# One sequence of hop groups, hop products head by head, and mix turned inside the base product, in an mLSTM attention and expert FFN kernel

## The chip, the cores and the metric

The kernel runs on one core of a Trainium2 chip. The metric is device time in microseconds, from start to end of one execution; the median of three runs of the kernel before is 4010.18 us.

## What is computed

For 32 batches of 512 queries and contexts of width 512, eight heads of 64: the query tokens are normalized; keys and values come from the context. The part that matters here is the hop term. Every pair (v, m) of positions has its own embedding row, looked up in a table of 2017 rows by an index matrix, and each query is multiplied with the rows of its 512 partners, head by head:

```python
pos_emb = rpe[hops]                                   # 512 x 512 indices, rows of 512
pe = pos_emb.reshape(Sq, Sq, NH, DH)
k_hop = jnp.einsum('bhvc,vmhc->bhvm', qh, pe)
qk = jnp.einsum('bhsd,bhtd->bhst', qh, k_scaled)
C = (qk + k_hop) * D                                  # D: causal decay, zero for m > v
normalizer = jnp.maximum(jnp.abs(jnp.sum(C, axis=-1, keepdims=True)), jnp.exp(-max_log_D))
h = (C / (normalizer + EPS)) @ vh                     # then a layer norm per head
```

Behind it stands a feed-forward part on x plus the attention output: a layer norm, a base product of 512 x 512, and a router that picks two of ten experts from ten scores and weights a low-rank product of rank 16 for each of eight true ones (128 columns in all). These weighted 128 columns are called mix; mix times a 128 x 512 matrix is added to the base product.

## The kernel before

All engines run their own list of instructions, tied together by semaphores. The span has a setup (to about 43 us), the hop stage (43 to about 1600 us) and the batch loop.

**The hop stage** computes k_hop for all batches at once and stores it in DRAM (hop_products). A group is four queries v with all 32 batches, 128 rows. Queries fall into four tiles of 128 (s = 0 to 3), each tile into four quarters of 32 (c) and each quarter into eight groups (k), 128 groups in all. Only partners m up to the query are needed, so a group of tile s has s full tiles of 128 partners for each of its four queries, and on the diagonal c + 1 tiles that hold 32 partners of each of the four queries. Its width is 128 s + 32 (c + 1) columns.

For each such tile GpSimd issues one indirect DMA (L661 for full tiles, L654 for diagonal ones) that gathers 128 table rows of 2 KB. Full tiles of query v go to rows[v], one buffer set of three tiles for each v; diagonal ones to rows_diag, two sets taken by the parity of c. GpSimd waits until PE has turned the former content. PE transposes each gathered tile in four instructions (L1246) into one of three PSUM banks; VectorE and ScalarE copy the tiles in turn (L484 diagonal, L487 full) to rowsT. Then the product of query v (L1261): the weights are the normalized queries of the group, turned by PE (L1215) and copied by ScalarE in two halves (L760) into q_diag, in which each pair of heads stands as a block of 64 columns with zeros in the rows of the other head. Four matmuls of 128 rows and 64 columns (a float32 matmul is two instructions) write two PSUM banks, which VectorE and ScalarE copy to hop_out (L496); SP stores hop_out in two DMAs for each group.

The order of a group is written out in hop_order: its diagonal tiles, the full tiles of queries 0 and 1, then product v followed by the full tiles of query v + 2. The statistics and the norm of the next group's queries (L953 to L960, L733, L735) stand in the same order. x of the group two ahead is loaded by four DMAs on SP (L525), queued behind the stores of the group before. hop_segments runs the four tiles s as four segments one after another, each with stages and semaphores of its own (pe_h, dve_h, act_h, gathered); at a seam GpSimd waits until the last tile of the segment before has been turned, and PE until its last copies are made. Inside a segment the order is k, then c.

**The batch loop** runs 32 batches as overlapping rounds of 12 steps. In a step PE forms scores of a unit (L1332), adds the hop products by transposing them into the same banks (L1340), weighs values with the unit before (L1356), and does the preparation of the next batch and the FFN of the one before between. SP loads the hop products (hop_load) for pairs of heads. DVE's router (L1119 to L1143) ends in mix; PE turns mix (turn_mix, L1373), ScalarE copies it to mixT (L898), and base (L1387, eight instructions, then L1389 with mixT, two) forms the base product. Four of these, t = 0 to 3, fall in each round. In the steps of BASE, turn_mix stands ahead of turn_context(2), turn_queries(0) and base. ScalarE runs in order: behind the copy to mixT stand the exponentials of the next unit (L810), which GpSimd masks (L687, L683) and DVE multiplies with the scores (L1054).

Of the kernel before, what the change touches and what calls it, by code (L numbers as in the profile page):

```python
# [52 lines left out]

class TwoRounds:
# [26 lines left out]
def build(nc, x, ctxt, hops, igate_w, igate_b, fgate_w, fgate_b, rpe, ln_w, ln_b,  # L81
# [14 lines left out]

# [23 lines left out]
    with ExitStack() as ctx:  # L120
# [38 lines left out]
        q_diag = [place(KT * VG * 2 * B) for _ in range(2)]  # L159
# [72 lines left out]
        act_q = Stage(sem("act_q"), ["ln", "rstd", "lo", "hi"])  # L232
        gathered = [[sem(f"gathered{s}_{v}") for v in range(VG)] for s in range(ST)]
        gathered_diag = [[[sem(f"gathered_diag{s}_{i}_{j}") for j in range(3 + i)] for i in range(2)] for s in range(ST)]
# [6 lines left out]
        def turn_steps(s, c, v):  # L241
            return [("turn", c, v, t) for t in range(s)]

        def diag_steps(c):
            return [("diag", c, j) for j in range(c + 1)]

        def hop_order(s, c):

            order = diag_steps(c) + turn_steps(s, c, 0) + turn_steps(s, c, 1)
            for v in range(VG):  # L250
                order.append(("prod", c, v))
                if v + 2 < VG:
                    order += turn_steps(s, c, v + 2)
            return order

        quarters = range(QUARTERS)


        turned_tiles = [[o for c in quarters for o in hop_order(s, c) if o[0] != "prod"] for s in range(ST)]
        turned_number = [{o: n for n, o in enumerate(ts)} for ts in turned_tiles]  # L260

        def evacuated_by(s, step, part):
            return step[0] == "prod" or turned_number[s][step] % 2 == part

        def turn_bank(s, step):
            return bank(TURN_BANKS[turned_number[s][step] % len(TURN_BANKS)])

        def bank_before(s, step):

            n = turned_number[s][step]  # L270
            n_banks = len(TURN_BANKS)
            if n >= n_banks:
                return turned_tiles[s][n - n_banks], 0
            return [o for m, o in enumerate(turned_tiles[s]) if m % n_banks == n][-1], 1

        pe_h, dve_h, act_h = [], [], []
        for s in range(ST):
# [155 lines left out]
        block = ctx.enter_context(nc.Block())  # L433


        def segment_over(engine, s, *stages):

            if s:
                for st in stages:
# [11 lines left out]
        def hop_segments(engine, body, apart=(ST - 1,), begin=None):  # L451

            for s in range(ST):
                if begin:
                    begin(s)
# [1008 lines left out]
```

## Time and profile before

| | |
|---|---|
| median of three runs | 4010.18 us (4005.64 to 4011.32) |
| profiled execution, time | 4004.49 us |
| its span | 4002.8 us |
| mean granted clock of PE | 0.954 of full speed |
| busy over the span | PE 86%, DVE 66%, ACT 46%, POOL 51% |
| moved | 813.64 MB, mean 203 GB/s |

The profiled execution is read for all durations. The span is what the rows below count from 0; the time is 1.7 us more. Matmuls of a line overlap each other, so for PE the busy time of a group divided by its count is the cost of one in the stream, and the mean of one is its latency. Indirect DMAs on POOL are the time in which GpSimd issues them.

### The profile page before, as it was taken

The numbers are of one execution on the slowest core, as the hardware profiler recorded it, in microseconds if no ns is written. First come the engines' busy times: TensorE is split into PE (matmuls) and PEld (weight loads), VectorE is DVE, ScalarE is ACT, GpSimd is POOL, SyncE is SP. The second block draws the span as 40 slices with busy tenths as digits, with TensorE's granted clock in tenths as the row PEclk, the third lists the DMA queues.
The fourth block names the chain that finished last, engine by engine and source line by source line (L and its number), as shares of the span: only waits on it lengthen the run. The fifth ranks groups of instructions, "written<-read, shape, count | busy, mean of one in ns | idle before, by whom it ended". The sixth has DMA issues, their size and how long they took to land.

```text
span 4002.8 us, 62357 instructions
## 1 busy us (share of the span) xinstructions
PE 3430.6 (86%) x20788; PEld 2029.9 (51%) x20788; DVE 2628.1 (66%) x5500; ACT 1838.8 (46%) x4353; POOL 2054.3 (51%) x2247
## 2 busy tenths in 40 slices
PE   4677878888788888589999999999999999999997
PEld 3555555555455454345555555555555555555543
DVE  5444545555444444477877888878888788887874
ACT  2444444444344444344444454545545455454441
POOL 2356667777777776134444444444444444444443
PEclk7789989999999999799999999999999999999998
DMA  5678889999899998455554544555545554555541
GB/s 143 194 225 285 290 268 328 326 339 335 289 335 326 331 329 302 143 160 146 148 151 143 161 138 139 168 152 157 144 140 166 151 159 142 145 164 147 166 120 36
DMA packets 409649, 813.64 MB, mean 203 GB/s; under 512 B 100314, under 2 KB 204762, under 8 KB 407284
## 3 DMA queue, kind: packets, MB, share of 16 engines
q1 hardware_dynamic: 322292, 524.36, 42.7%
q0 software_dynamic: 87040, 285.28, 22.1%
q8 instruction: 171, 2.80, 0.3%
q14 instruction: 146, 1.20, 0.1%
HBM read 632.67 MB, written 176.69 MB: 202 GB/s over the span
## 4 chain that ended last, share of the span: by engine, by line
PE 41%; DVE 21%; DMA 14%; issue 8%; ACT 6%; POOL 5%; SPq 4%; DVEq 0%; ACTq 0%; POOLq 0%
PE psum L1387 11%; PE psum L1261 7%; DMA arena<-in_L_xattn_rpe_dram,arena 6%; PE psum L1246 5%; DMA arena<-in_x_dram 5%; POOL arena L661 4%; DVE arena L1054 4%; PE psum L1340 4%; PE psum L1332 3%; PE psum L1310 3%; DMA arena<-hop_products 3%; PE psum L1389 3%; PE psum L1279 2%; SPq L525 2%; ACT arena L810 2%
## 5 line engine op out<-in xcount | busy, mean ns | idle before, releaser
L661 POOL DMA_INDIRECT arena<-in_L_xattn_rpe_dram,arena x768 | 730.0, 951 | 290.5 <-issue 180.6
L1246 PE MATMUL psum<-arena 128*128 128x128 f32 x4352 | 619.5, 291 | 230.6 <-DMA arena<-in_L_xattn_rpe_dram,arena 126.7
L1246 PEld LDWEIGHTS psum<-arena 128*128 128x128 f32 x4352 | 499.0, 148 | 430.6 <-issue 210.9
L1261 PE MATMUL psum<-arena 128*64 128x32 f32 (+7 forms) x4096 | 599.0, 427 | 69.0 <-ACT arena L484 41.8
L687 POOL TENSOR_SCALAR_AFFINE_SELECT arena<-arena 128x256 f32<-128x256 f32 x256 | 112.4, 439 | 891.0 <-ACT arena L810 722.1
L496 DVE COPY arena<-psum 128x32 f32<-128x32 f32 (+15 forms) x512 | 226.6, 443 | 443.9 <-PE psum L1261 439.8
L810 ACT ACTIVATE arena<-arena 128x512 f32<-128x512 f32 (+3 forms) x1024 | 503.3, 561 | 3.8 <-DMA arena<-gate_rows 3.8
L1387 PE MATMUL psum<-arena 128*128 128x512 f32 x1024 | 477.0, 610 | 17.6 <-ACT arena L795 17.6
L1054 DVE TENSOR_TENSOR arena<-psum,arena 128x1024 f32<-128x1024 f32 (+1 forms) x384 | 397.6, 1041 | 120.3 <-PE psum L1340 115.4
L487 DVE COPY arena<-psum 128x512 f32<-128x512 f32 x384 | 265.8, 692 | 278.8 <-PE psum L1246 278.0
L654 POOL DMA_INDIRECT arena<-in_L_xattn_rpe_dram,arena x320 | 304.7, 952 | 261.8 <-issue 141.5
L1261 PEld LDWEIGHTS psum<-arena 128*64 128x64 f32 x4096 | 258.6, 149 | 294.1 <-issue 190.2
L1340 PE MATMUL psum<-arena 128*128 128x128 f32 x2560 | 366.3, 282 | 29.0 <-DMA arena<-hop_products 29.0
L1279 PE MATMUL psum<-arena 128*128 128x128 f32 x2176 | 329.3, 282 | 68.4 <-DVE arena L999 27.1
L496 ACT COPY arena<-psum 128x32 f32<-128x32 f32 (+15 forms) x512 | 193.9, 388 | 412.9 <-PE psum L1261 408.3
L1332 PE MATMUL psum<-arena 64*128 64x512 f32 (+3 forms) x2048 | 382.2, 471 | 0.0
L1340 PEld LDWEIGHTS psum<-arena 128*128 128x128 f32 x2560 | 274.9, 141 | 186.0 <-issue 122.6
L1356 PE MATMUL psum<-arena 128*64 128x512 f32 (+3 forms) x2048 | 359.9, 451 | 1.5 <-DVE arena L1054 1.5
L1279 PEld LDWEIGHTS psum<-arena 128*128 128x128 f32 x2176 | 243.8, 142 | 217.4 <-issue 134.6
L487 ACT COPY arena<-psum 128x512 f32<-128x512 f32 x384 | 226.7, 590 | 252.0 <-PE psum L1246 249.8
L1387 PEld LDWEIGHTS psum<-arena 128*128 128x128 f32 x1024 | 190.2, 196 | 214.8 <-issue 214.1
L733 ACT ACTIVATE arena<-arena 128x1 f32<-128x1 f32 x384 | 111.9, 291 | 342.6 <-DVE arena L955 209.9
(104 smaller groups left out, 4883.6 us busy)
## 6 DMA issues: line engine op xcount, KB each, us to landing
arena<-in_x_dram SPq DMA_DIRECT2D x256, 256.0 KB, 3.6
arena<-gate_rows SPq DMA_DIRECT2D x128, 512.0 KB, 4.3
arena<-in_x_dram SPq DMA_DIRECT2D x512, 64.0 KB
arena<-in_ctx_dram SPq DMA_DIRECT2D x32, 1024.0 KB, 7.9
out_dram<-arena SPq DMA_DIRECT2D x128, 256.0 KB, 2.5
arena<-in_L_xattn_rpe_dram,arena POOLq DMA_INDIRECT x1088, 5.7
hop_products<-arena SPq DMA_DIRECT2D x16, 1024.0 KB
arena<-hop_products SPq DMA_DIRECT2D x128, 128.0 KB, 3.0
```

The lines of the kernel that those rows point to most:

```text
L487: copy(rowsT[c % 2][:, o[2], :, o[3] * P:(o[3] + 1) * P], turn_bank(s, o).rearrange("p (k m) -> p k m", k=KT)).then_inc(stage.sem, stage.s ...
L496: copy(hop_out[c][:, lo:lo + width], bank(3 + 2 * (v % 2) + i, width)).then_inc(stage.sem, stage.step(o))
L661: nc.gpsimd.indirect_dma_start(out=rows[v][:, t, :], out_offset=None, in_=rpe[:, :], in_offset=bass.IndirectOffsetOnAxis(ap=here[:, t, v:v ...
L810: last = nc.scalar.activation(decay[u % 3][:, e, at:at + width], top_pair[p % 2][:, e * S + j * P:e * S + j * P + width], ACT.Exp, bias=st ...
L1054: nc.vector.tensor_tensor(scoresT[u % 2][:, :, 0:width], got[:, :, 0:width], decay[u % 3][:, :, 0:width], ALU.mult).then_inc(dve_a.sem, dv ...
L1246: last = nc.tensor.transpose(turn_bank(s, o)[:, q * P:(q + 1) * P], own[:, q * P:(q + 1) * P], ident)
L1261: last = nc.tensor.matmul(psum[j * 64:(j + 1) * 64, (3 + 2 * (v % 2) + i) * BANK:(3 + 2 * (v % 2) + i) * BANK + width], qd[:, 2 * i + j, v ...
L1279: last = nc.tensor.transpose(bank(b)[:, k * P:(k + 1) * P], src[:, k * P:(k + 1) * P], ident)
L1332: nc.tensor.matmul(psum[:, at[e] + col:at[e] + col + width], kT[ra.par][half, p, j * P:(j + 1) * P], qT[ra.par][half, p, j * P:j * P + width],
L1340: last = nc.tensor.matmul(psum[:, at[e] + n * P:at[e] + (n + 1) * P], hop_in[p % 2][:, e, Q_OFF[i] + j * P:Q_OFF[i] + (j + 1) * P], ident, ...
L1356: last = nc.tensor.matmul(psum[e * DH:(e + 1) * DH, 4 * BANK + j * P:4 * BANK + j * P + width], values[ra.par][:, j, HPT * p + e, :], scor ...
L1387: nc.tensor.matmul(bank(6), ffn_xT[t % 2][:, k, :], base_wT[:, k, :], start=(k == 0), stop=False)
```

## The change

Three things are changed.

First, the segments are dissolved. A list GROUP orders all 128 groups in one sequence: first the groups of tiles 3 and 0, then those of tiles 2 and 1, and inside each half the tiles take turns over the quarters, c running 0 to 3 as before (3,0,3,0 and then 0,3,0,3 for each k). The engines wait on plain counters (Line) in place of stages by segment; the waits at the seams are gone. Buffers, banks and the order inside a group are as before. The x load of two groups ahead goes by the new order.

Second, the hop product of a query is formed head by head: eight matmuls with 64 rows and 32 columns of weights, each to its own 32 partitions, even and odd heads in two banks. The queries are kept as PE turned them (q_turned), copied by one instruction; q_diag and its zeros are gone. Rows of a head lie at another place in hop_products, and hop_load is changed accordingly.

Third, turn_mix is called inside base, between its second and third k step; before, it stood ahead of turn_context(2), turn_queries(0) and base.

```diff
+        GROUP = []
+        for two in ((3, 0), (2, 1)):
+            for k in range(BODIES):
+                for first in range(2):
+                    GROUP += [(two[(c + first) % 2], c, k) for c in quarters]
...
-        hop_load = [[d.rearrange("(p e b) v m -> p b v e m", b=B, e=HPT) for d in ds] for ds in hop_dram]
+        hop_load = [[d.rearrange("(e p b) v m -> p b v e m", b=B, e=HPT) for d in ds] for ds in hop_dram]
...
+            for n in range(GROUPS):
+                s, c, k = GROUP[n]
+                width = VG * hop_width(n)
+                if n + 2 < GROUPS:
+                    sp.wait_ge(dve_q.sem, dve_q.done(n, "norm"))
+                    load_group(n % 2, rows_of(n + 2))
+
+                sp.wait_ge(*act_h.at(("prod", n, VG - 1)))
...
+                if n >= 2:
+                    pool.wait_ge(*pe_h.at(diag_steps(n - 2)[-1]))
+                for j in range(c + 1):
+                    nc.gpsimd.indirect_dma_start(
+                        out=rows_diag[c % 2][:, j, :], out_offset=None, in_=rpe[:, :],
...
+                for v in range(VG if s else 0):
+
+                    if tiles_before(n) is not None:
+                        pool.wait_ge(*pe_h.at(turn_steps(tiles_before(n), v)[-1]))
+                    for t in range(s):
...
-                dst = q_diag[par].rearrange("p (k e b) -> p k e b", e=2, b=B)
-                for e, name in enumerate(("lo", "hi")):
-                    rows_e = slice(e * DH, (e + 1) * DH)
-                    nc.scalar.copy(dst[rows_e, :, e, :], src[rows_e]).then_inc(act_q.sem, act_q.step(name))
+                nc.scalar.copy(q_turned[par], bank(QUERY_BANK)).then_inc(act_q.sem, act_q.step("copy"))
...
-                            for i in range(2):
-                                for j in range(2):
-                                    last = nc.tensor.matmul(
-                                        psum[j * 64:(j + 1) * 64,
-                                             (3 + 2 * (v % 2) + i) * BANK:(3 + 2 * (v % 2) + i) * BANK + width],
-                                        qd[:, 2 * i + j, v, :], rowsT[c % 2][:, v, 2 * i + j, 0:width],
-                                        start=True, stop=True)
+                        for p in range(KT):
+                            for e in range(HPT):
+                                at = (3 + 2 * (v % 2) + e) * BANK
+                                half = slice(e * DH, (e + 1) * DH)
+                                last = nc.tensor.matmul(
+                                    psum[p * B:(p + 1) * B, at:at + width],
+                                    qt[half, p, v, :], rowsT[c % 2][half, v, p, 0:width], start=True, stop=True)
...
                     for k in range(KT):
+                        if k == KT // 2:
+                            turn_mix(r, t)
                         nc.tensor.matmul(bank(6), ffn_xT[t % 2][:, k, :], base_wT[:, k, :], start=(k == 0), stop=False)
...
-                    for t, r in due(BASE, s, rf, rg):
-                        turn_mix(r, t)
```

## Rows read from the trace of the kernel before

**Rows 1.** The page: PE and DMA, busy tenths in 40 slices of 100 us.

```profile
PE   4677878888788888589999999999999999999997
...
DMA  5678889999899998455554544555545554555541
```

**Rows 2.** Stages: length; PE, PEld, DVE, ACT, POOL busy us (count); clock; DMA share; GB/s.

```profile
43.00:251.00 208.00, 144.13 (x1442) 115.12 (x1442) 97.77 (x263) 97.64 (x294) 76.74 (x81) 0.78 0.64 189
251.00:574.00 323.00, 260.09 (x2012) 181.10 (x2013) 156.22 (x330) 149.11 (x363) 198.51 (x209) 0.92 0.86 279
574.00:1006.00 432.00, 362.81 (x2492) 233.68 (x2488) 216.53 (x392) 200.62 (x423) 319.01 (x336) 0.95 0.96 325
1006.00:1597.00 591.00, 484.86 (x3008) 294.44 (x3008) 277.16 (x454) 252.63 (x487) 440.43 (x464) 0.95 0.94 322
1612.00:4002.00 2390.00, 2167.52 (x11776) 1197.39 (x11776) 1851.36 (x3969) 1135.73 (x2784) 1018.83 (x1152) 0.98 0.50 145
```

**Rows 3.** GpSimd's timeline: start, us, line; first gathers of segments 0, 1, 3; idle before.

```profile
43.33 1.13 POOL L654 DMA_INDIRECT arena<-in_L_xattn_rpe_dram,arena  x1 [41.38 <-issue]
...
250.96 0.95 POOL L654 DMA_INDIRECT arena<-in_L_xattn_rpe_dram,arena  x1 [10.94 <-issue]
252.21 0.94 POOL L661 DMA_INDIRECT arena<-in_L_xattn_rpe_dram,arena  x1 [0.31 <-issue]
...
1006.95 0.94 POOL L654 DMA_INDIRECT arena<-in_L_xattn_rpe_dram,arena  x1 [8.33 <-issue]
```

**Rows 4.** Groups by line, hop stage: busy us, mean ns; idle before and releaser.

```profile
L661 POOL DMA_INDIRECT arena<-in_L_xattn_rpe_dram,arena x768 | 730.0, 951 | 290.5 <-issue 180.6 <-PE psum L1246 93.8 <-PE psum L1261 16.1
...
L654 POOL DMA_INDIRECT arena<-in_L_xattn_rpe_dram,arena x320 | 304.7, 952 | 261.8 <-issue 141.5 <-PE psum L1246 116.0 <-PE psum L1261 4.3
...
L1261 PE MATMUL psum<-arena 128*64 128x512 f32 x256 | 64.9, 641 | 0.0
...
L1261 PE MATMUL psum<-arena 128*64 128x32 f32 (+7 forms) x4096 | 599.0, 427 | 69.0 <-ACT arena L484 41.8 <-DVE arena L487 10.1 <-DVE arena L484 9.6
```

**Rows 5.** Waits in segment 0 (L654, L953) and segment 1 (L661): total us, times, longest.

```profile
POOL arena L654 <- PE psum L1246: 105.0, 30, 8.9
...
DVE arena L953 <- DMA arena<-in_x_dram: 25.6, 12, 4.8
...
POOL arena L661 <- PE psum L1246: 70.0, 60, 2.9
```

**Rows 6.** DMA queues, 574 to 1006 us: packets, MB, share; landing, 1006 to 1597.

```profile
q0 software_dynamic: 26880, 88.10, 62.1%
q1 hardware_dynamic: 15360, 51.92, 33.3%
...
arena<-in_L_xattn_rpe_dram,arena POOLq DMA_INDIRECT x464, 5.5
```

**Rows 7.** Groups by shape in the batch loop, 1612 to 4003 us.

```profile
L1332 PE MATMUL psum<-arena 64*128 64x512 f32 x512 | 145.5, 645 | 0.0
...
L1356 PE MATMUL psum<-arena 128*64 128x512 f32 x512 | 138.2, 618 | 0.0
```

**Rows 8.** PE's waits in the batch loop, and the group of mixT's copy.

```profile
PE psum L1373 <- DVE arena L1143: 94.2, 96, 5.4
...
PE psum L1387 <- ACT arena L795: 17.6, 30, 0.9
...
L898 ACT COPY arena<-psum 128x128 f32<-128x128 f32 x128 | 33.6, 263 | 80.2 <-PE psum L1373 80.2
```

**Rows 9.** PE's timeline: first base product of a round; mix before the other three.

```profile
2614.01 3.67 PE L1387 MATMUL psum<-arena 128*128 128x512 f32 x8 [0.58 <-ACT arena L795]
...
2632.32 0.33 PE L1373 MATMUL psum<-arena 128*128 128x128 f32 x1 [0.23 <-DVE arena L1143]
...
2648.81 0.33 PE L1373 MATMUL psum<-arena 128*128 128x128 f32 x1 [0.59 <-DVE arena L1143]
...
2667.34 0.33 PE L1373 MATMUL psum<-arena 128*128 128x128 f32 x1 [1.74 <-DVE arena L1143]
```

More of the change, by code:

```diff
@@ L51, in inc, with __init__, at @@
         return self.sem, self.step(name)
+class Line:
+    def __init__(self, sem, steps):
+        self.sem, self.steps = sem, list(steps)
+        self.number = {s: n + 1 for n, s in enumerate(self.steps)}
+        self.taken = 0
+    def inc(self, name):
+        assert self.steps[self.taken] == name, (name, self.steps[self.taken])
+        self.taken += 1
+        return self.sem, 1
+    def at(self, name):
+        return self.sem, self.number[name]
 class TwoRounds:
@@ L158, in build @@
         x_stats = place(8)
-        q_diag = [place(KT * VG * 2 * B) for _ in range(2)]
+        q_turned = [place(KT * VG * B) for _ in range(2)]
         diag_lists = place(ST * QUARTERS * BODIES * QUARTERS).bitcast(I32).rearrange(
@@ L239, in build @@
         QUERY_BANK = 7
[L241 to L249, printed above, removed]
+        quarters = range(QUARTERS)
+        GROUP = []
[3 more added lines that the diff above has]
+                    GROUP += [(two[(c + first) % 2], c, k) for c in quarters]
@@ L448, in hops_over @@
             engine.wait_ge(pe_q.sem, pe_q.done(GROUPS - 1, "turn"))
-            engine.wait_ge(act_q.sem, act_q.done(GROUPS - 1, "hi"))
[L451 to L455, printed above, removed]
-                for k in range(BODIES):
-                    body(s, k, k == BODIES - 1 and s in apart and s == ST - 1)
+            engine.wait_ge(act_q.sem, act_q.done(GROUPS - 1, "copy"))
         def rounds(run):
@@ L477, in batch_loop, with hop_copy @@
             body(0, B + 1, "g")
-        def hop_copy(engine, copy, stages, s, k, o, part):
-            stage, c = stages[s], o[1]
-            engine.wait_ge(pe_h[s].sem, pe_h[s].done(k, o))
+        def hop_copy(engine, copy, line, o, part):
+            n = o[1]
+            s, c, k = GROUP[n]
+            engine.wait_ge(*pe_h.at(o))
             if o[0] == "diag":
@@ L738, in _ @@
             act_q.start(act)
-            for s in range(ST):
-                act_h[s].start(act)
             for st in (act_p, act_a, act_o, act_n, act_f):
@@ L912, in _ @@
             dve_q.start(dve)
-            for s in range(ST):
-                dve_h[s].start(dve)
             for st in (dve_p, dve_a, dve_o, dve_f):
@@ L1195, in _ @@
             pe_q.start(pe)
-            for s in range(ST):
-                pe_h[s].start(pe)
             for st in (pe_p, pe_a, pe_o, pe_f):
```

266 lines of the change are left out of this document (113 added, 153 removed).

## The prediction, made before the change was run

> **What bounds the kernel now.** I read the page first. Two stages stand apart in its slices [rows 1]: until about 1600 us the DMA engines are nearly full and PE is not; from there to the end PE is in the highest class and DMA is half used. The stage table gives this in numbers [rows 2]: the four segments of the hop stage (one for each query tile s = 0, 1, 2, 3) and the batch loop behind them. Then I took GpSimd's timeline at the seams of the segments [rows 3], the groups by shape [rows 4], who released GpSimd [rows 5], the DMA queues [rows 6], and last the batch loop: groups, PE's waits, and PE's timeline around the four base products of a round [rows 7 to 9].
>
> In the hop stage GpSimd issues 768 + 320 = 1088 row gathers. Undisturbed, one starts 1.25 us after the last (250.96 to 252.21) [rows 3]; 1088 of them are 1363 us. The first starts at 43.3 and the last ends before 1597, 1554 us. So 191 us of that are not gathers. The segments divide it: segment 0 has 80 gathers (100 us) in 208; segment 1 has 208 (260 us) in 323; segment 2 has 336 (421 us) in 433; segment 3 has 464 (581 us) in 590. Idle: 108, 63, 12, 9. The three seams hold 10.9 (the first) to 8.3 us (the last), about 28 of it [rows 3]; the rest is in segment 0 (105 us waiting for PE's turning of diagonal tiles, which hold two buffer sets) and in segment 1 (70 us waiting for PE to free the row buffers) [rows 5]. Segments 2 and 3 are bound by GpSimd's issue, with DMA at 96 and 94% close behind; segments 0 and 1 by the latency of the loop between PE, the evictions and the gathers, while GpSimd and DMA have room. That is what alternating tiles can level.
>
> In the batch loop PE is busy 2168 of 2390 us [rows 2]; the rest is waits, of which 94 us stand at L1373, the turning of mix, behind DVE's router (L1143), in 96 of 128 cases [rows 8].
>
> **Change part by part.**
>
> *One sequence, 3 with 0 and 2 with 1.* No gather, transfer or byte is added or taken. A pair of groups has 17 gathers on average in both halves, 21.3 us at 1.25. What PE needs for a pair must stay below that. From [rows 2]: segment 3 has 485 us of PE work in 32 groups, 15.2 each; segment 0 144/32 = 4.5; sum 19.7, and 16 to 17 once the products shrink (below). For 2 and 1: 363/32 + 260/32 = 19.5, then about 16. So the pair is bound by the gathers, with some 5 us of room. What is left of the 191 us of idle time: (a) the rate at which segment 3 already runs, 9 us in 581, gives 20 on 1363. (b) The order is 3,0,3,0,0,3,0,3, so once in eight groups two tile-0 groups stand together. There GpSimd has only 4 + 1 diagonal gathers (6.3 us) before it must wait for PE to have turned the diagonals of two groups back. PE gets there a landing of 5.5 us [rows 6], three transposed tiles (1.5 us), two products (2) and four diagonal tiles (2 to 3) after the last row gather: about 12. So 5 to 6 us, eight times: 45. (c) In 2,1,1,2 the single row buffers are reused after fewer gathers: about 1 us at two places of each eight groups, 16 us. The three seams (28 us) are gone. That makes 1363 + 81 = 1444.
>
> The other limit is DMA. The packets' time of the two queues over the four stages, in shares of the engines: in the 574 to 1006 stage 62.1 + 33.3% [rows 6] for 26,880 + 15,360 packets. That is 88.1 MB of gathers in 268 us, 3.04 us per MB, and 51.9 MB of stores and x loads at 2.77. The hop stage moves 1088 x 0.262 = 285 MB of gathers and 176 MB on the other queue, 867 + 488 = 1355 us. At the 96 to 97% that this queue reached, 1400; and GpSimd's stalls are partly DMA's too. I take **1450 us for 1554: 104 less**. Bounds: 191 less (no stall) and nothing (each group keeps its latency, next part).
>
> The x load of two groups ahead is queued on SP behind the stores of the group before; in segment 0 it made DVE wait 12 times, 25.6 us in all [rows 5]. Behind a short tile-0 group it will be late again, 2 to 3 us, and DVE holds evictions behind it. While PE has 5 us of room per pair this hides under the gathers; uncovered, 64 x 2 = 128 us, which would eat the gain.
>
> *Products head by head.* 8 products of 64 rows x 32 columns for 4 of 128 x 64, in 16 instructions for 8. An instruction over 512 columns now takes 64.9/256 = 0.253 us of busy time and the mean of all is 599/4096 = 0.146 [rows 4]. Beside each other on column halves (L1356, 138.2/512 = 0.270) or on row halves (L1332, 145.5/512 = 0.284), two run at once [rows 7], since one alone takes 0.46 (eight base instructions in 3.67 us [rows 9]). No row shows row halves and four column groups together. If all eight tiles run at once, 16 instructions need half the time of today's 8: 599 becomes 300, plus some cost of starting, say 350. If only two run at once it becomes 8192 x 0.146 = 1196. I take 350, nearer to the rows, which show both directions running two at once. While GpSimd binds, the 250 us that PE saves are not on the path; they are the room above. ACT loses one of its two query copies and DVE two memsets of the setup, both off the path: 0.
>
> The Trainium skill, page "TensorE: Matmul & The Clock Gate", section "Part 3: Packing small matmuls", says that row and column tiling compose, 10.6 times at sixteen tiles. By it, the products would be at the 300 us end; the same section calls matmuls strictly first-in first-out, and by that alone the second pass of one tile would hold back the next tile, 16 products' passes in series, near the 1196 end. No row of before decides between the two for eight tiles.
>
> *mix turned inside the base product.* The transpose (0.33 us) moves behind two of four k steps of the base product. Eight base instructions take 3.67 us, so 1.8 us of work now lies ahead of the wait. In a round the four turnings of mix wait under 0.1, 0.23, 0.59 and 1.74 us today [rows 9]. All are under 1.8, so they vanish. But before the first of the four, base itself waits for ACT's copy (L795, 17.6 us in all [rows 8]; 0.58 at 2614.01 [rows 9]), which is not moved; there the transpose, now inside the product, costs 0.16 us instead. Sum 0.23 + 0.59 + 1.74 - 0.16 = 2.4 us, x 32 batches = 77. What comes back: the wait for mixT has two k steps (1.8 us) of cover in place of four, for ACT's copy of 0.26 us [rows 8] that can stand behind an exponential; and ACT, in order, waits at L898 up to 1.8 us longer, with the next unit's exponentials behind it, for which GpSimd's mask and DVE's product wait. I take 12 us: **65 less**. Bounds: 94, and 0 if DVE's router is simply met later.
>
> **Sum.** The profiled execution: 4004.5 - 104 - 65 = 3835.5. The median of the runs is 5.7 us above the profiled one (4010.2): 3841, so **3840**.
>
> **Rivals.**
> A, both gains as above, 3840 (3790 to 3890): 0.57.
> B, GpSimd's stream has almost no stall and the batch loop gives all: 4010 - 170 - 85 = 3755 (to 3790): 0.12. For it: segment 3 idles 9 us in 590. Against: two full resources at once, and (b).
> C, the hop stage gains little, 4010 - 20 - 65 = 3925 (3890 to 3990): 0.17. Mechanisms: late x loads, or the clock. PE's granted clock was 0.78 in the stage where PE was 69% busy, 0.95 where it was 82 to 84% [rows 2]. With shorter products PE is busy 16 of 22.6 us, 71%. At 0.78 a pair's 16 us become 19.5, and with the landing latencies the loop is longer than the gathers by 1 to 2 us: +60 to 130. The Trainium skill has this rule on the same page ("Part 1: The HAM clock gate"): a PE with idle gaps is throttled to half rate. It is a rule against making PE's work shorter, and the stage of segment 0 agrees.
> D, the other side: the eight tiles do not run together. With 0.146 us an instruction PE's work in the hop stage grows by 597 us, 1252 (the four stages of [rows 2]) to 1849, plus the gaps it has, about 1900: 350 more, less 65, 4290. It decides from the point at which the hop stage eats the batch loop's gain: PE work up by some 400 us, 0.12 us an instruction. Chance 0.09.
> E, nothing moves, since the stalls reappear elsewhere (within 0.2%): 0.03; and slightly slower by the same: 0.02.
>
> **Chances.** About 0.2% (8 us) is what a measurement of this kernel can tell from no change. Faster 0.86, same 0.03, slower 0.11. The range holds A, most of B, and C up to 3925: 3765 to 3925.
>
> **What would show it.** L1246's and L1261's rows: L1261 x8192 at 300 to 400 us busy shows the eight tiles; 1100 or more shows D. GpSimd's first to last gather in 1450 us, with waits of 5 to 6 us on PE once in eight groups of the 3/0 half; DMA share even at 95% where it now climbs from 64 to 96. The clock in the hop stage at 0.9 or more; at 0.8, C. In the batch loop the wait at the turning of mix gone, PE's wait for mixT under 10 us, and 2325 us for 2390. If DVE's wait for x grows over 100 us, the load order was the wrong thing to dismiss.

## The result, and the profile after

The changed kernel takes 3946.36 us (median of four runs, 3941.99 to 3959.78) where the kernel before takes 4007.91 on the same chip: ratio 0.9854, 95% interval 0.9825 to 0.9882. That is 62 us faster; 3840 was forecast with a range of 3765 to 3925, so the time lies 21 us outside. The profiled execution's span is 3940.2 us, PE's mean clock 0.926.

The stages of the changed kernel: the half of tiles 3 and 0, the half of 2 and 1, the batch loop. Columns as in [rows 2].

```profile
45.00:857.00 812.00, 530.14 (x6412) 376.72 (x6412) 364.51 (x707) 303.74 (x708) 516.96 (x544) 0.81 0.85 281
857.00:1584.00 727.00, 551.16 (x6556) 354.31 (x6556) 373.83 (x725) 314.10 (x725) 518.00 (x544) 0.89 0.96 320
1600.00:3939.00 2339.00, 2161.82 (x11776) 1196.43 (x11776) 1875.52 (x3973) 1136.03 (x2784) 1000.31 (x1152) 0.98 0.51 148
```

From the page, PE, its clock and DMA in 40 slices, now of 98.5 us, to hold beside [rows 1].

```profile
PE   4666666667777777589999999999999999999998
...
PEclk8788888878888988699999999999999999999999
DMA  5888888889999999455555554555545545555451
```

The gathers run from 45.0 to 1582.9 us: 1538 us from first start to last start. In the kernel before they run from 43.3 to 1587.9, 1545 us; the 1554 of the prediction counted to the end of the stage. So the hop stage gave 7 us and not 104. The rest of the span, behind the last gather, fell from 2414.8 to 2357.3 us: 57.5, of 65 forecast. With the 1.7 us by which the first gather now starts later taken off, these two make up the 62.6 by which the spans differ. DMA's share is 0.85 in the first half and 0.96 in the second: it did not become even.

Who waited, total us, times, longest. Over the span, DVE's statistics of x (L946, once L953) and GpSimd's diagonal and full gathers:

```profile
DVE arena L946 <- DMA arena<-in_x_dram: 243.0, 62, 8.3
...
POOL arena L665 <- PE psum L1232: 120.9, 34, 16.5
...
POOL arena L674 <- PE psum L1232: 94.2, 107, 4.5
```

DVE now waits 243 us for x, where it waited 68 before (26 of them in segment 0 [rows 5]). The groups of the hop stage by line, transposes and products:

```profile
L1232 PE MATMUL psum<-arena 128*128 128x128 f32 x4352 | 693.6, 315 | 335.1 <-ACT arena L503 119.3 <-DMA arena<-in_L_xattn_rpe_dram,arena 116.0 <-DVE arena L503 99.2
...
L1248 PE MATMUL psum<-arena 64*32 64x416 f32 (+7 forms) x8192 | 363.2, 426 | 119.0 <-ACT arena L740 53.6 <-ACT arena L503 34.1 <-DVE arena L506 10.7
```

The products' busy time is 363 us for 8192 instructions, 0.044 us each, for 0.146 before [rows 4]. Last, PE's waits in the batch loop, to hold beside [rows 8]:

```profile
PE psum L1320 <- DMA arena<-hop_products: 37.1, 18, 8.5
PE psum L1385 <- ACT arena L899: 36.6, 35, 1.2
PE psum L1369 <- ACT arena L792: 29.0, 30, 1.0
...
PE psum L1353 <- DVE arena L1133: 6.0, 4, 3.7
```

### The profile page after: what moved, and what is told of

It is laid out like the page before. It is cut to its first block, busy times and chain, and to the rows that moved or that the text cites. A ratio compares the mean times of both kernels' runs of the same rounds, so it can differ in the third digit from the quotient of the medians.

```text
span 3940.2 us, 70397 instructions
## 1 busy us (share of the span) xinstructions
PE 3260.7 (83%) x24884; PEld 1940.2 (49%) x24884; DVE 2641.2 (67%) x5498; ACT 1758.8 (45%) x4225; POOL 2036.1 (52%) x2247
## 4 chain that ended last, share of the span: by engine, by line
PE 40%; DVE 20%; DMA 18%; SPq 6%; issue 6%; ACT 6%; POOL 3%; DVEq 0%; ACTq 0%; POOLq 0%
PE psum L1232 8%; PE psum L1369 8%; DMA arena<-in_x_dram 7%; DMA arena<-in_L_xattn_rpe_dram,arena 6%; PE psum L1248 5%; DVE arena L1044 4%; DMA arena<-hop_products 4%; PE psum L1320 4%; SPq L543 4%; PE psum L1312 3%; PE psum L1336 3%; PE psum L1290 3%; POOL arena L674 3%; PE psum L1259 2%; ACT arena L807 2%
## 5 line engine op out<-in xcount | busy, mean ns | idle before, releaser
L1232 PE MATMUL psum<-arena 128*128 128x128 f32 x4352 | 693.6, 315 | 335.1 <-ACT arena L503 119.3
L1232 PEld LDWEIGHTS psum<-arena 128*128 128x128 f32 x4352 | 570.5, 162 | 553.1 <-issue 341.8
L1369 PE MATMUL psum<-arena 128*128 128x512 f32 x1024 | 489.7, 607 | 29.0 <-ACT arena L792 29.0
L1044 DVE TENSOR_TENSOR arena<-psum,arena 128x1024 f32<-128x1024 f32 (+1 forms) x384 | 397.7, 1041 | 111.5 <-PE psum L1320 110.4
L1248 PE MATMUL psum<-arena 64*32 64x416 f32 (+7 forms) x8192 | 363.2, 426 | 119.0 <-ACT arena L740 53.6
L515 DVE COPY arena<-psum 128x416 f32<-128x416 f32 (+15 forms) x512 | 224.7, 442 | 269.9 <-PE psum L1248 265.0
L1320 PE MATMUL psum<-arena 128*128 128x128 f32 x2560 | 368.0, 283 | 37.3 <-DMA arena<-hop_products 37.1
L1259 PE MATMUL psum<-arena 128*128 128x128 f32 x2176 | 335.8, 285 | 70.3 <-DVE arena L989 24.6
L1320 PEld LDWEIGHTS psum<-arena 128*128 128x128 f32 x2560 | 276.3, 142 | 194.7 <-issue 116.4
L1259 PEld LDWEIGHTS psum<-arena 128*128 128x128 f32 x2176 | 247.3, 144 | 227.2 <-issue 115.2
L515 ACT COPY arena<-psum 128x416 f32<-128x416 f32 (+15 forms) x512 | 199.9, 390 | 274.6 <-PE psum L1248 266.6
L1369 PEld LDWEIGHTS psum<-arena 128*128 128x128 f32 x1024 | 175.5, 191 | 207.8 <-issue 194.1
L946 DVE BATCH_NORM_STATS2 arena<-arena 128x6 f32<-128x512 f32 x128 | 88.1, 688 | 243.1 <-DMA arena<-in_x_dram 243.0
```

The lines of the kernel that those rows point to most:

```text
L515: copy(hop_out[c][:, lo:lo + width], bank(3 + 2 * (v % 2) + i, width)).then_inc(*line.inc(o))
L1044: nc.vector.tensor_tensor(scoresT[u % 2][:, :, 0:width], got[:, :, 0:width], decay[u % 3][:, :, 0:width], ALU.mult).then_inc(dve_a.sem, dv ...
L1232: last = nc.tensor.transpose(turn_bank(o)[:, q * P:(q + 1) * P], own[:, q * P:(q + 1) * P], ident)
L1248: last = nc.tensor.matmul(psum[p * B:(p + 1) * B, at:at + width], qt[half, p, v, :], rowsT[c % 2][half, v, p, 0:width], start=True, stop=True)
L1259: last = nc.tensor.transpose(bank(b)[:, k * P:(k + 1) * P], src[:, k * P:(k + 1) * P], ident)
L1320: last = nc.tensor.matmul(psum[:, at[e] + n * P:at[e] + (n + 1) * P], hop_in[p % 2][:, e, Q_OFF[i] + j * P:Q_OFF[i] + (j + 1) * P], ident, ...
```

## The experiments

**What was asked.** Theory: the hop stage lost its gain to late x loads, the thing that the prediction had named and dismissed. SP queues the load of group n + 2 behind the stores of group n - 1, which wait for that group's last product. Rivals: PE's clock fell (0.81 in the first half); the meetings of two tile-0 groups; and the smaller products do not help. Most runs are from chips on which the kernel before takes 4006 to 4010 us, and they come first; seven are from two chips on which it takes 4256 and 4259, and they have a part of their own.

**The load moved, and the load left out.** The first run changes the place of the loads alone:

```diff
-                if n + 2 < GROUPS:
-                    sp.wait_ge(dve_q.sem, dve_q.done(n, "norm"))
-                    load_group(n % 2, rows_of(n + 2))
+                if n + 3 < GROUPS:
+                    sp.wait_ge(dve_q.sem, dve_q.done(n + 1, "norm"))
+                    load_group((n + 1) % 2, rows_of(n + 3))
```

(and group 2 is loaded ahead of the loop). The second leaves out all x loads behind the first two groups.

> The changed kernel, with the x load of group n + 3 issued as soon as the norm of group n + 1 is done, ahead of the stores of group n, in place of behind the stores of the group before. Theory (late x loads took the hop gain): DVE's wait for x, 243 us in the changed kernel, falls under 80 us, gathers run from 45 to about 1500 us in place of 1584, and the time is about 3870 us. Rival (the two adjacent tile-0 groups with two diagonal buffer sets, or the lower clock of 0.81): DVE's wait for x falls as well, but GpSimd's wait for the diagonal tiles stays at 100 us or more and the time is 3930 us or more.

> The changed kernel without the x loads behind the first two groups; the hop products of the other groups are formed from the x of these two. It leaves out 33 MB of loads and every wait for them. Theory (late x): within 15 us of the kernel with early loads, at 3850 to 3870 us, since only their lateness counts. Rival (the share of DMA that they take, or the buffers for diagonal tiles): if DMA bandwidth is what they cost, it is another 30 us or more below the kernel with early loads; if the buffers are, it stays at 3920 us or more.

Measured: 3850.5 us (ratio 0.9614, interval 0.9581 to 0.9648) with the load moved, 3846.5 without it. So 96 of the 106 us by which the time missed the forecast come from the place of four DMA issues on SP in each group, and there is almost nothing left to gain from x. The first run was expected at about 3870, so the move gave 20 us more than its theory had it. Stages of the first run, and GpSimd's waits over the hop stage:

```profile
43.80:780.50 736.70, 532.10 (x6432) 364.50 (x6433) 366.67 (x713) 306.82 (x713) 516.54 (x545) 0.84 0.92 311
780.50:1490.70 710.20, 546.31 (x6538) 343.55 (x6536) 369.49 (x719) 313.21 (x720) 515.38 (x544) 0.90 0.96 326
```

```profile
POOL arena L667 <- PE psum L1234: 69.0, 48, 7.6
...
POOL arena L676 <- PE psum L1234: 62.7, 111, 4.1
```

The gathers take 1447 us from first to last. In the 3/0 half GpSimd's stops beyond its usual 0.3 us between gathers, summed group by group from the trace, are 54.2 us, and all of them stand at the eight places behind two tile-0 groups (in the changed kernel: 132.8 us, 110.4 of them at these places). The clock is 0.84 and 0.90 in the two halves, hardly above the changed kernel's 0.81 and 0.89, and still the stage comes out where it was forecast: the clock was not what held it.

**The parts by themselves.** The move of mix alone, in the kernel before:

```diff
                     for k in range(KT):
+                        if k == KT // 2:
+                            turn_mix(r, t)
...
-                    for t, r in due(BASE, s, rf, rg):
-                        turn_mix(r, t)
```

> The kernel before with the turning of mix moved inside the base product, and nothing else. Theory (the batch loop alone gave the measured gain of 61 us): 50 to 65 us below the kernel before, PE's wait at the turning of mix from 94 to under 10 us. Rival (part of the loop's gain comes from the other layout of the stored hop products): 30 us or less.

Measured: 3954.6 us, 0.9877 (0.9841 to 0.9914), 52 less than the 4006.4 of the same chip, all of it behind the last gather. PE's waits there:

```profile
PE psum L1340 <- DMA arena<-hop_products: 41.5, 19, 8.8
PE psum L1405 <- ACT arena L902: 36.6, 35, 1.2
PE psum L1389 <- ACT arena L795: 29.9, 30, 1.3
...
PE psum L1373 <- DVE arena L1143: 7.0, 5, 3.7
```

The head products alone, in the order of the segments (q_turned, the eight matmuls and hop_load's order of rows as in the change's diff):

> The kernel before, in its four segments, with the products head by head and the new layout of the stored products, and nothing else. Theory (segments 2 and 3 are bound by the gathers; 0 and 1 by latency to which the product adds little): 20 to 40 us less, all in segments 0 and 1, product group at 350 us busy for 599. Rival (a lower clock eats what PE saves): within 10 us of the kernel before, the granted clock of segments 0 and 1 lower by 0.05 or more.

Measured: 3973.1 us, 0.9917 (0.9886 to 0.9949), 33 less. The stage of the gathers shrank by 23, all of it in segments 0 and 1 (10.5 and 12.1 us), as the theory had it. PE's groups there, products and transposes:

```profile
L1240 PE MATMUL psum<-arena 128*128 128x128 f32 x4352 | 674.8, 307 | 351.1 <-DMA arena<-in_L_xattn_rpe_dram,arena 256.9 <-ACT arena L484 57.4 <-DVE arena L484 36.1
...
L1257 PE MATMUL psum<-arena 64*32 64x32 f32 (+7 forms) x8192 | 382.3, 447 | 80.0 <-ACT arena L484 37.3 <-DVE arena L487 12.0 <-ACT arena L735 10.1
```

And the order alone (turns, one sequence, late loads, with products and mix as before):

> The same kernel as e8 (the new sequence of groups alone, x loads late, old products, mix where it was). On a chip where the kernel before takes about 4006 us: theory (late x takes what the order gives): within 20 us of 4006, DVE's wait for x 200 us or more. Rival (with the longer products x arrives in time): under 3970 us. A third way, seen on the other chip: slower by 50 us or more, since there the old products leave no room.

Measured: 4055.4 us, 1.0116 (1.0099 to 1.0133), near the third way of what was expected. **The order by itself makes the kernel slower by 49 us.** Its gathers take 1607 us, and these are the waits:

```profile
DVE arena L952 <- DMA arena<-in_x_dram: 211.1, 58, 7.8
...
POOL arena L665 <- PE psum L1238: 154.4, 35, 20.8
...
POOL arena L674 <- PE psum L1238: 136.5, 119, 6.3
```

The three parts, +49, -33 and -52, sum to -36, and the change gave -62: the products are worth more in the late-load order (4055.4 less the 52 of mix is 4003; the changed kernel has 3946, so 57) than in segments. Their room hiding a part of the stops would explain it, and the table below fits that.

**Order with early loads.** Is the turning of tiles worth anything once x is in time? Three kernels with early loads: the segments' order in one sequence, the changed kernel's order with only its loops exchanged so that two tile-0 groups meet once and not eight times, and the changed kernel's order with the old products.

```diff
-        for two in ((3, 0), (2, 1)):
-            for k in range(BODIES):
-                for first in range(2):
-                    GROUP += [(two[(c + first) % 2], c, k) for c in quarters]
+        for s in range(ST):
+            for k in range(BODIES):
+                GROUP += [(s, c, k) for c in quarters]
```

```diff
         for two in ((3, 0), (2, 1)):
-            for k in range(BODIES):
-                for first in range(2):
+            for first in range(2):
+                for k in range(BODIES):
                     GROUP += [(two[(c + first) % 2], c, k) for c in quarters]
```

> The same kernel as e5 (early x loads, one sequence, but in the order of the four segments). On a chip where the kernel before takes about 4006 us: theory (taking turns levels the gathers): gathers 1490 us or more in place of 1447, 3885 us or more. Rival (the early x load alone gave the gain): within 10 us of 3850.

> The same kernel as e7 (early x loads, the smaller tile's groups meet once in a half). On the chip of e5 to e8 both it and the kernel before ran 250 us or more longer in the hop stage, so the order is asked again. On a chip where the kernel before takes about 4006 us: theory (the wait for the diagonal sets at eight meetings in a half is worth 35 to 45 us): about 3815 us, gathers about 1410 us. Rival (DMA binds by then): 3835 us or more, gathers 1430 us or more.

> The same kernel as e6 (early x loads, turns taken, old products). On a chip where the kernel before takes about 4006 us: theory (the gathers bind, with room for the old products): 3850 to 3875 us, gathers 1447 to 1470 us. Rival (the shorter products made the room): 3900 us or more, gathers 1500 us or more.

Measured: segments 3856.0 us (0.9613), one meeting 3814.4 (0.9521, interval 0.9505 to 0.9537), old products 3877.6 (0.9674). So turns in the change's order are worth 5 us over the segments, within what the runs scatter; with one meeting they are worth 42. That refutes the theory for the segments (3885 or more), bears out the one for one meeting (3815), and leaves the old products just above their theory (3850 to 3875). The one-meeting kernel is the fastest of all, 192 us under the kernel before. Its first half and its wait for the diagonals (the latter 69.0 us, 48 times in the run with eight meetings):

```profile
45.00:735.00 690.00, 518.09 (x6435) 357.64 (x6436) 367.18 (x712) 308.26 (x714) 516.82 (x545) 0.88 0.98 331
735.00:1459.00 724.00, 547.14 (x6535) 350.13 (x6533) 369.26 (x719) 313.72 (x720) 514.63 (x544) 0.89 0.93 321
```

```profile
POOL arena L667 <- PE psum L1234: 15.9, 28, 7.7
...
POOL arena L676 <- PE psum L1234: 81.4, 123, 2.7
```

By the same count as above, GpSimd's stops fall from 54.2 to 7.4 us in the 3/0 half and rise from 29 to 43 in the 2/1 half; the 33 us between are the gain in the gathers (1447 to 1414).

The old products in the early order cost 27 us (3877.6 for 3850.5), with PE busy 573 us in them:

```profile
L1255 PE MATMUL psum<-arena 128*64 128x416 f32 (+7 forms) x4070 | 572.8, 412 | 59.3 <-ACT arena L503 33.1 <-DVE arena L503 9.9 <-DVE arena L506 7.2
```

**Late loads in other orders.** What was left is whether the turns made the loads late or they were late already. Three kernels: the changed one with late loads in the order of the segments; the kernel before with early loads (the same move of the loads, across its seams too); the changed one with late loads and one meeting.

> The changed kernel with late x loads and the groups in the order of the four segments, no turns, once more, since the chip of the run before is one on which the kernel before takes 4259 us. Where the kernel before takes about 4007: by the theory that the turns make the late loads costly, 3915 (3905 to 3925); by the rival that late loads cost the same in any order, 3945, with x waits of about 240 us.

> The kernel before with its x loads alone moved ahead of the stores, once more. On the chip where the kernel before takes 4259 us it gave 11 us. Where it takes about 4007: theory 30 to 50 us, 3955 to 3975; rival, GpSimd's other waits take its place, 3990 or more, after the run on the other chip the likelier.

> The changed kernel with late x loads and the loops over k and first exchanged, once more. Where the kernel before takes about 4007: by the theory that the meetings' price adds to that of the late loads, 3910 (3900 to 3920); by the rival that the late loads already stop everything there, 3935 to 3950.

Measured, with 4009.8 us for the kernel before: 3914.7 us (0.9758), 3936.5 (0.9816, interval 0.9795 to 0.9838) and 4009.1 (0.9992, 0.9980 to 1.0004). The first met its number, the second gained 73 us where 30 to 50 were expected, and the third went against both theory and rival: with late loads the order that is best with early ones loses 63 us to the changed kernel. DVE's wait for x, first in the segments, then with one meeting:

```profile
DVE arena L945 <- DMA arena<-in_x_dram: 83.7, 34, 5.0
```

```profile
DVE arena L946 <- DMA arena<-in_x_dram: 354.1, 63, 9.5
```

All of it in one table, medians in us, on chips where the kernel before takes 4006 to 4010; behind each late one DVE's wait for x in its trace.

| kernel | late loads | DVE waits for x | early loads | given by the move |
|---|---|---|---|---|
| before | 4009.8 | 68 | 3936.5 | 73 |
| order of the change, old products (late: old mix too) | 4055.4 | 211 | 3877.6 | 126, and 52 for mix |
| changed, in segments | 3914.7 | 84 | 3856.0 | 59 |
| changed | 3946.4 | 243 | 3850.5 | 96 |
| changed, one meeting | 4009.1 | 354 | 3814.4 | 195 |

The column of waits grows with the places where a tile-0 group follows one of tile 3: none in the segments, 24 in the changed kernel's first half, 31 with one meeting (and there are 31 waits there, 7.8 us each). In the changed kernel 161 of that half's 172 us of waits stand at these 24 places. The kernel before with early loads goes through its segment 0 in 174 us for 208 [rows 2], with GpSimd's waits for the diagonals (L655, over all segments) at

```profile
POOL arena L655 <- PE psum L1247: 83.0, 66, 5.4
```

Its second and third seams are still there; below, GpSimd's timeline at them, then at the same places of the one sequence in segments with early loads:

```profile
501.52 0.94 POOL L655 DMA_INDIRECT arena<-in_L_xattn_rpe_dram,arena  x1 [7.93 <-issue]
...
931.65 0.95 POOL L655 DMA_INDIRECT arena<-in_L_xattn_rpe_dram,arena  x1 [7.79 <-issue]
```

```profile
487.52 0.94 POOL L666 DMA_INDIRECT arena<-in_L_xattn_rpe_dram,arena  x1 [0.30 <-PE psum L1233]
...
909.71 0.95 POOL L666 DMA_INDIRECT arena<-in_L_xattn_rpe_dram,arena  x1 [0.30 <-issue]
```

The timeline of the late kernel with one meeting shows a place where a tile-0 group follows one of tile 3 (start us, us, engine, line; idle before and releaser):

```profile
420.33 0.43 SPq L560 DMA_DIRECT2D hop_products<-arena  x1
420.81 5.55 SPq L543 DMA_DIRECT2D arena<-in_x_dram  x4
...
423.94 0.67 PE L1248 MATMUL psum<-arena 64*32 64x128 f32 x32
...
424.90 0.45 PE L1248 MATMUL psum<-arena 64*32 64x128 f32 x16 [0.30 <-ACT arena L515]
...
433.67 0.69 DVE L946 BATCH_NORM_STATS2 arena<-arena 128x6 f32<-128x512 f32 x1 [7.92 <-DMA arena<-in_x_dram]
...
434.61 0.30 ACT L738 ACTIVATE arena<-arena 128x1 f32<-128x1 f32 x1 [8.88 <-DVE arena L948]
435.21 3.68 PE L1232 MATMUL psum<-arena 128*128 128x128 f32 x16 [8.39 <-DVE arena L503]
436.60 0.95 POOL L674 DMA_INDIRECT arena<-in_L_xattn_rpe_dram,arena  x1 [5.80 <-PE psum L1232]
```

At 420.33 SP issues the second store of the long group, half a microsecond later the four x loads, whose issue alone takes 5.55 us on the queue. The short group between is through its last product by 425.4. DVE reaches the next statistics and waits 7.9 us, in front of its evictions; so PE waits 8.4 for a bank, and GpSimd 5.8 for its buffers. By the landings that the trace holds for these loads, this one took 12.8 us from first issue to last landing. The median of that is 11.4 us in this half, 11.0 in the changed kernel's, 8.3 with the load ahead of the stores, and 5.1 in segment 0 of the kernel before, where DMA is busy 0.64 of the time [rows 2]. In the changed kernel it is 10.9 behind a short group's stores and 11.3 behind a long group's (two of 832 to 1024 KB each), and in the kernel before it goes up with the segments, 5.1, 8.5, 10.6 and 12.1, as DMA's share and the stores both grow. How much of it the stores in front make and how much the full DMA engines, these numbers do not part. So the load is slow nearly everywhere, and late where the group between is short. When the group between is a long one (12 us and more of PE's stream, as from 406.7 to 420), a load of 11 us is barely seen.

**The other kind of chip.** Seven kernels first ran on chips where the kernel before takes 4256.1 (four of them) and 4259.2 us (three).

> The kernel with early x loads, its groups in the order of the four segments again (0, 1, 2, 3) but in one sequence. Theory (taking turns levels the gathers): the idle time of GpSimd in tiles 0 and 1 comes back, gathers run for about 1490 us in place of 1447, and the time is 3885 us or more. Rival (it was the early x load alone that gave the gain, whatever the order): within 10 us of 3850.

> The kernel with early x loads and turns taken, with the old products of 128 rows x 64 columns. Theory (the gathers bind, and PE has room of 1.5 us for a pair of groups even with the old products): gathers 1447 to 1470 us, 3850 to 3875 us. Rival (PE's latency sets the pace and the shorter products made the room): gathers 1500 us or more, 3900 us or more; the granted clock is higher than with the new products in both cases.

> The kernel with early x loads, with the two loops over k and over which tile begins exchanged, so that two groups of the smaller tile stand together once in a half in place of eight times. Theory (GpSimd's wait for the diagonal buffer sets at these places is 5 to 6 us each, as the prediction had it): gathers 35 to 45 us shorter than 1447, GpSimd's wait at the diagonal gathers from 69 to under 35 us, 3810 us. Rival (DMA, at 96% and more, takes the place): gathers no shorter than 1430, 3835 us or more.

> The kernel before with the new sequence of groups alone: old products, mix where it was, x loads late. Theory (late x takes what the order gives): DVE's wait for x 200 us or more, gathers 1530 to 1560 us, within 20 us of the kernel before. Rival (with the longer products the groups are long enough for x to arrive): DVE's wait under 150 us and 40 us or more faster.

These have the edits of the segments, old products and one meeting with early loads, and of the order alone. Measured: 4339.3 (1.0213), 4332.5 (1.0175), 4295.0 (1.0083, interval 1.0059 to 1.0107) and 4476.4 us (1.0515, interval 1.0474 to 1.0556). The three others, whose edits are those of the three "late loads" kernels above:

> The changed kernel with its late x loads, its products, its mix and its one sequence without seams, but the groups in the order of the four segments (0, 1, 2, 3), no turns. Theory: taking turns is what makes the late loads costly, because a long group's stores stand ahead of the load for a short one in half of all places; without turns only segment 0 waits for x, so hop stage about 1508 us from first to last gather, time 3915 (3905 to 3925), and DVE waits for x under 100 us in all where the changed kernel has 243. Rival: the late loads cost the same in any order, since every group has them: 3945, x waits about 240 us.

> The kernel before with one thing changed: x of group n + 3 is loaded right behind the norm of group n + 1, ahead of the stores of group n, also across the seams. Theory: the late load was already a cost of the kernel before, mostly in segment 0 (DVE waited 68 us for x in all, GpSimd 105 us for the diagonal tiles), so moving it gives 30 to 50 us, time 3955 to 3975. Rival: in the kernel before GpSimd's other waits (two buffer sets of diagonal tiles) take its place, under 10 us gained: 3998 or more.

> The changed kernel with its late x loads, and only the loops over k and first exchanged in its order, so that two groups of tile 0 meet once in the 3/0 half and not eight times. Theory: the meetings' price is of its own and adds to that of the late loads, as it did with the loads early (36 us): 3910 (3900 to 3920), DVE's waits for x over 200 us. Rival: the meetings cost little here, because the late loads already stop everything at those places: 3935 to 3950.

Measured: 4325.9 (1.0163), 4248.2 (0.9978, 0.9967 to 0.9990) and 4385.4 us (1.0306). Nearly every number expected was missed, since they had been worked out for the other chips. The trace of the one-meeting kernel with early loads shows where these chips differ (DVE's waits, then two rows of the timeline):

```profile
DVE arena L515 <- remote: 327.4, 91, 15.7
DVE arena L515 <- PE psum L1250: 249.3, 211, 5.5
DVE arena L515 <- PE psum L1234: 228.9, 127, 5.7
```

```profile
902.24 0.69 DVE L515 COPY arena<-psum 128x512 f32<-128x512 f32 x1 [2.95 <-PE psum L1234]
...
905.15 0.69 DVE L515 COPY arena<-psum 128x512 f32<-128x512 f32 x1 [2.23 <-remote]
```

DVE's copies of the products wait 806 us in all, where the same kernel on the other chip has 259 for PE's product. 327 of it is labelled "remote": no instruction in the profile ends close to the release. But the trace holds the semaphores, and all 91 of these waits ended with an update of PE's own hop counter, which only PE's matmuls raise, half of them 3.0 us or more after the end that the profile gives the last of these matmuls. So in every part of the 806 us the copies wait for PE. PE is busy 1300 us in the hop stage for 1065, and its granted clock is 0.79 for 0.89. Whether the clock is the cause or falls because PE waits, no run tells. The batch loop has its usual length (2360 us behind the last gather). Of the orders, one meeting is the better there too when x is early (4295 for 4339 in segments) and the worse when x is late (4385 for 4326). Why PE's work comes later there in the hop stage is open: there is a place and a size, no cause.

## Why the prediction was wrong, and where it was right

**The step that failed** is the one on the x load: "While PE has 5 us of room per pair this hides under the gathers". Its facts were right: the load is late behind a short group, DVE holds evictions behind it, and uncovered it would eat the gain. Two things were wrong. The size: 5.4 us each in the 3/0 half (171.8 us, 32 times), not 2 to 3, since behind the stores and with DMA full the load takes 11 us to land and not the 5 of segment 0, where I had read the delay. Segment 3 of the kernel before already had 12, covered by its long groups. And the room: 5 us per pair is a mean over 21 us. As I read the timeline above, it exists only while gathered rows are lying ready and GpSimd has buffers free, and a stop of DVE empties both at once, since full rows have one set and diagonal ones two. That is read from one such place; no run varied the number of sets. What the room did hide can be read off the table: with the new products 40% of the wait for x reached the time in the changed kernel (96 of 243), 55% with one meeting (195 of 354), 70% in segments (59 of 84); with the old ones 60% in turns (126 of 211), and in the kernel before all of it (73 for 68). So the room took off at most 60% of the waits. These shares are rough: in segment 0 of the kernel before the move gave 34 us where DVE had waited 26, so the wait is not all that a late load costs.

**1450 us for the gathers** was right for the kernel that the prediction had in mind: 1447 with early loads, and the meetings stood where they were put. They were priced at 45 us and took 54.2; taking seven of eight away gave 36 (3850.5 to 3814.4). The turns of 2 and 1 took 29 for 16. That the sum came out is in part luck, since term (a) had no ground: the 9 us of idle in segment 3 are the time behind its last gather, which starts at 1587.9, and its 464 gathers take 582 us at 581 undisturbed. For the same reason 104 was too much: against the 1545 us from first to last start, 1450 gives 95.

**"That is what alternating tiles can level"** was half right. The idle time of segments 0 and 1 was read rightly, 108 and 63 us, but a part of it was the late load's: in the kernel before, the early load alone takes segment 0 from 208 to 174 us and segment 1 from 323 to 285, and gives 73 in all. What stays can be levelled, but the turns bring idle time of their own. With x early the segments have 66 and 17 us of it in tiles 0 and 1, 83 in all; the change's order has as much, mostly at its eight meetings, and is as fast (3850.5 for 3856.0). With one meeting 51 us are left, and only there turns pay, by 42 us.

**The seams** at 28 us were right in size. The kernel before with early loads still has 8.6, 7.9 and 7.8 us at them, the one sequence in segments 1.1, 0.3 and 0.3, and its gathers are 22 us shorter, 6.5, 7.4, 7.9 and 0.3 by segment. With late loads the one sequence has 16 us less in its gathers than the segments with the new products (1505.1 for 1521.5). In the medians the parts do not add up so well: from 3936.5 to 3856.0 is 80.5 us, less than 52 for mix, 27 for the products and 22 for the seams. No run has the new products with seams and early loads, so what seams and products give apart is known to some 20 us only.

**The products**: 350 us busy forecast, 363 measured. By the prediction's own measure, 0.146 us an instruction with two at once, 0.044 is between six and seven at once, so the eight tiles do run together ([rows 7] had shown two at once in either direction). The rule of the Trainium skill, page "TensorE: Matmul & The Clock Gate", section "Part 3: Packing small matmuls", that row and column tiling compose is borne out by 599.0 to 363.2 us with twice the instructions. Its first-in first-out sentence is about the order in which matmuls start and end while they overlap; it does not say that tiles run one after another, and so it was no ground for the rival at 4290. That they give nothing on the path was too modest: 27 us in the early order, 33 in segments with late loads. That a shorter product brings the turned rows, and so free buffers, sooner would explain it; this is argued, not shown.

**mix**: 65 forecast, 52 alone and 57.5 in the change. PE's wait on the router fell from 94.2 to 6.0 us, 88 where 82 was taken (2.56 us in 32 batches). What came back was larger than the 12: base's own wait rose by 11.4 us (29.0 for 17.6), the router's product (L1385) waits 36.6 for ACT's copy of xT where it waited 17.3, since on ACT that copy stands behind the copy to mixT, and the wait for hop_products has 8 more. The product with mixT itself never waits.

**Rivals and chances.** C held the mechanism, "late x loads, or the clock", at 3925 with 0.17; the time was 21 us above its middle and inside its own 3890 to 3990. The range was cut at its middle, which is the second error: the priced case should have gone in whole. Of C's two mechanisms the loads did it. The clock did fall to 0.81, and at 0.84 the early kernel reached 1447 us all the same. The rule of the Trainium skill on the same page (section "Part 1: The HAM clock gate"), a PE with idle gaps is throttled, agrees with that fall; it did not bring the cost that C had put on it. D (eight tiles in series) fell. The sign, at 0.86, was right.

## What to carry to other kernels

When work of different lengths is interleaved, look at every transfer that is queued behind another one's completion: its lead is the length of the shortest piece in between, not the mean. Read its time to land where the queue and the DMA engines are as full as they will be. A stop on an engine that holds evictions passes to the others, so an average of free time hides only a part of it, here none to 60%. And before an order is changed to fill idle time, ask what a moved load alone would give: that alone gave 73 us in the kernel before, more than the whole change.

## What the runs showed of the hardware

Chips run the same program 6% apart: the kernel before takes 4006 to 4010 us on most and 4256 and 4259 on two. It was not traced on these two. In the seven kernels that were, the gathers take 315 to 466 us more than in the same kernel on the other chips, and the rest of the span differs by 16 us at most: the kernel before with early loads takes 1783 us for its gathers in place of 1468, and the one-meeting kernel 1880 in place of 1414, with DVE's copies of products waiting 806 us for PE in place of 259. The same edit can be worth 73 us on the one (0.9816) and 11 on the other (0.9978), and the change's products, mix and sequence, in segments with late loads, win 95 us on the one and lose 67 on the other. The four x loads of a group, 256 KB, take 5.1 us from issue to landing where DMA is busy 0.64 of the time behind small stores, and 12.1 where it is busy 0.94 behind large ones. And 64x32 tiles in float32 cost 0.044 us an instruction at eight tiles together, the mean over all widths, at a clock of 0.81 to 0.89.
